# Cross attention of a two-layer decoder: the constant with which Pool rounds the probabilities, and the products that took it out again

## The reference, cut to what matters

```python
def _fq_unsigned(x, axis):
    s = jnp.max(x, axis=axis, keepdims=True) / 255.0
    s = jnp.maximum(s, 1e-08)
    q = jnp.clip(jnp.round(x / s), 0.0, 255.0) * s
...
attn = jnp.einsum('bhqd,bhkd->bhqk', q, k)
attn = jax.nn.softmax(attn.astype(jnp.float32), axis=-1)
attn = _fq_unsigned(attn, axis=-1)
out = jnp.einsum('bhqk,bhkd->bhqd', attn, v)
```

## Time and profile before

| | us |
|---|---|
| median of 3 runs | 1989.98 |
| their range | 1984.67 to 1989.99 |
| the profiled execution | 1981.8 |
| its span in the trace | 1980.1 |

### The profile page before, as it was taken

One profiled execution on the slowest core, in us unless ns is written; L12 is line 12 of the kernel. 1 busy time (PEld: TensorE's weight loads), 2 busy tenths in 40 slices (PEclk: granted clock), 3 DMA queues, 4 the chain that ended last, 5 costly groups with the idle time before them and its releaser, 6 DMA issues. The chain is left out here.

```text
span 1980.1 us, 38681 instructions
## 1 busy us (share of the span) xinstructions
PE 1809.8 (91%) x15222; PEld 968.5 (49%) x15222; DVE 1349.2 (68%) x2353; ACT 1131.5 (57%) x1657; POOL 970.0 (49%) x1021
## 2 busy tenths in 40 slices
PE   7988999979999999999999999999999578899698
PEld 3476788846665333333333333333333367666454
DVE  1454777775667999999999999999600353676622
ACT  2170556645623777777777777777777253766311
POOL 1010455559702878878787887878878010000000
PEclk9998999979999999999999999999999775999889
DMA  6002444457664111111111011100010240465000
GB/s 220 0 1 55 116 121 120 114 148 173 189 195 122 25 25 21 25 25 21 17 25 25 13 25 25 24 13 1 17 38 28 62 129 1 131 178 166 30 1 10
DMA packets 105395, 132.20 MB, mean 67 GB/s; under 512 B 9047, under 2 KB 94875, under 8 KB 104860
## 3 DMA queue, kind: packets, MB, share of 16 engines
q1 hardware_dynamic: 104364, 128.39, 24.7%
q10 hardware_dynamic: 864, 1.51, 0.2%
HBM read 89.78 MB, written 38.55 MB: 65 GB/s over the span
## 5 line engine op out<-in xcount | busy, mean ns | idle before, releaser
L1127 DVE TENSOR_REDUCE c_top<-c_ps 128x1 f32<-128x500 f32 x1344 | 827.7, 672 | 83.9 <-PE c_ps L875 36.3
L795 POOL TENSOR_SCALAR c_values<-c_values 125x896 f16<-125x896 f32 x768 | 721.5, 939 | 265.3 <-ACT c_values L1343 231.8
L1343 ACT ACTIVATE c_values<-c_ps 125x896 f32<-125x896 f32 x768 | 660.7, 915 | 238.3 <-PE c_ps L952 237.9
L964 PE MATMUL c_ps<-c_values,c_total 125*32 125x448 f32 x3072 | 369.0, 551 | 1.5 <-POOL c_values L795 1.5
L875 PE MATMUL c_ps<-kx,c_qx 64*128 64x500 f16 x1152 | 316.0, 386 | 24.6 <-DVE c_top L1127 15.0
L952 PE MATMUL c_ps<-c_qx,kx 64*125 64x448 f16 x1536 | 252.7, 362 | 4.1 <-ACT c_values L1343 3.9
L875 PEld LDWEIGHTS c_ps<-kx,c_qx 64*128 64x128 f16 x1152 | 82.3, 93 | 289.5 <-DVE c_top L1127 232.7
L815 PE MATMUL c_ps<-shared_w,c_rows 128*125 128x256 f32 x768 | 184.7, 384 | 0.0
L815 PEld LDWEIGHTS c_ps<-shared_w,c_rows 128*125 128x125 f32 x768 | 146.1, 190 | 24.4
L969 PE MATMUL c_ps<-c_values 125*16 125x448 f16 x1536 | 143.8, 352 | 0.0
L2009 POOL MEMSET f_select<- 8x1408 f32 x1 | 1.3, 1262 | 286.5 <-POOLq L1705 286.5
(11 more groups left out here) (275 smaller groups left out, 2158.7 us busy)
## 6 DMA issues: line engine op xcount, KB each, us to landing
c_rows<-in_ctx_T SPq DMA_DIRECT2D x96, 250.0 KB, 3.5
kx<-k_parts SPq DMA_DIRECT2D x192, 93.8 KB, 3.7
v<-c_halves SPq DMA_DIRECT2D x48, 265.6 KB
c_v<-v SPq DMA_DIRECT2D x16, 796.9 KB
k_parts<-c_parts SPq DMA_DIRECT2D x48, 250.0 KB, 2.6
k_T<-c_kback SPq DMA_DIRECT2D x48, 250.0 KB, 5.7
c_kT<-k_T SPq DMA_DIRECT2D x16, 750.0 KB
f_wgu<-in_f_Wgu SPq DMA_DIRECT2D x2, 1408.0 KB, 19.2
```

The source lines that it names most:

```text
L795: nc.gpsimd.tensor_scalar(probs[:, n % SLOTS], expo[:, n % SLOTS], ROUND_AT, 1.0, ALU.add, ALU.mult).then_inc(s["rounded"], 1)
L964: nc.tensor.matmul(ps[32 * g:32 * g + 32, 3, 0:TOKENS], total[:], expo[:, n % SLOTS, g % 2, :], start=(at == 0), stop=False, skip_group_ch ...
L1127: nc.vector.tensor_reduce(top[:, pair % 2, tile, at:at + 1], ring(n)[:, 0:BLOCK], AX.X, ALU.max)\
L1343: nc.scalar.activation(expo[:, n % SLOTS], ps[0:KP, 4 + 2 * (n % 2):6 + 2 * (n % 2), 0:TOKENS], ACT.Exp, scale=UNSCALE, bias=LN255).then_i ...
```

## The change

ROUND_AT becomes 3 * 2^22 = 12582912. Pool now adds it and subtracts it in the same instruction; between 2^23 and 2^24 the f32 numbers are 1 apart, so the addition rounds and the subtraction leaves the step itself, which is written as f16. As the steps carry no offset, Pool's 42 additions of V's steps, PE's 192 offset products with their weight loads, PE's wait for them, and DVE's fill of `offset` go.

```diff
-ROUND_AT = 1024.0
+ROUND_AT = float(3 << 22)
...
-        offset = sb("c0_offset", [KP, TOKENS], F16)
...
-                link = linker(pool, s["vlink"])
-
-                def sum_values(group):
-                    pool.wait_ge(cs["v_steps"], 8 * group + 8)
-                    if group == 0:
-                        pool.wait_ge(cs["stored"], (UNITS // 2) * 32)
-                    tiles = v_steps[:, 16 * group:16 * group + 16, :].rearrange("p (j a) n -> p j a n", a=2)
-                    link(nc.gpsimd.tensor_tensor(v_sums[:, group], tiles[:, 0], tiles[:, 1], ALU.add))
-                    for j in range(2, 8):
-                        link(nc.gpsimd.tensor_tensor(v_sums[:, group], v_sums[:, group], tiles[:, j], ALU.add))
-
...
-                for group in range(KT // 16):
-                    sum_values(group)
...
-                    nc.gpsimd.tensor_scalar(probs[:, n % SLOTS], expo[:, n % SLOTS], ROUND_AT, 1.0,
-                                            ALU.add, ALU.mult).then_inc(s["rounded"], 1)
+                    nc.gpsimd.tensor_scalar(probs[:, n % SLOTS], expo[:, n % SLOTS], ROUND_AT, ROUND_AT,
+                                            ALU.add, ALU.subtract).then_inc(s["rounded"], 1)
...
-                    if at % 8 == 7:
-                        if b == 7:
-                            pe.wait_ge(s["vlink"], 7 * (KT // 16))
-                        for g in range(4):
-                            h = 2 * pair + g % 2
-                            last = nc.tensor.matmul(ps[32 * g:32 * g + HD, 3, 0:TOKENS],
-                                                    v_sums[:, at // 8, g // 2, h * HD:(h + 1) * HD], offset[:],
-                                                    start=False, stop=True, skip_group_check=True)
...
-                nc.vector.memset(offset[:], -ROUND_AT).then_inc(s["side_ones"], 1)
...
-                    dve.wait_ge(s["side_ones"], 3)
+                    dve.wait_ge(s["side_ones"], 2)
```

More of the change, by code:

```diff
@@ L554, in layer0_cross_attention @@
         ctx_T = late(128, 0, 896).rearrange("p (c n) -> p c n", c=C2)
-        v_sums = parts[0:KP].rearrange("p s i c n -> p (s i c n)")[:, 0:6 * 2 * D]\
-            .rearrange("p (g a n) -> p g a n", g=6, a=2)
         w = k.sum_all[:, 0:2 * D].rearrange("p (c n) -> p c n", c=C2)
```

## The result

| | median us | runs | range |
|---|---|---|---|
| before | 1987.79 | 4 | 1984.67 to 1989.99 |
| after | 3518.41 | 4 | 3514.72 to 3521.26 |

The ratio is 1.770 (95% interval 1.766 to 1.773): the kernel takes 1531 us more, where 8 us less were forecast. It is the rival that had 3 in 100, at a price beyond the far bound.

A forecast was written before the change was run, and what follows sets the result against it. The prediction took a loop of PE and DVE handing banks to each other as the bound, with offset products in PE's link. Gains of 7.8 + 0.2 = 8.0 us took 1990.0 to 1982.0 us, range 1972 to 1988.

The forecast's parts named there:

- the rival that had 3 in 100: Layer 0's cross attention: slower roundings make Pool the bound; about 2630 us at 2.018 us a rounding; chance 0.03.
- the far bound: Highest price considered for Pool's new rounding: 2018 ns for 896 elements, at the pace of Pool's tensor_tensor.
- The rounding itself: Pool's add and subtract in one tensor_scalar: taken at 939 ns, the price of add with multiply for 125x896.
- The point from which Pool decides, 1.13 us: Price of a rounding from which Pool sets the step; each 0.1 us beyond costs 77 us.
- PE's offset products while both passes run: 41 groups in PE's loop with DVE, 0.19 us gained for each that goes: 7.8 us, between nothing and 12.3.
- the last group: Offset products at the second pass's end, which ACT's copy of the bank waits for: 0.19 us gained.
- The second pass alone: Six groups of offset products after the first pass, lying in a wait for ACT's exp: nothing, at most 1.1 us.
- The sums of V's steps: Pool's 42 additions, 48 us, ending before Pool's 82 us wait for ACT: dropping them gains nothing.
- the fill of offset: DVE's 0.43 us fill, absorbed by a later 1.05 us wait for Pool: nothing gained, at most 0.43 us.
- Hidden after all: PE catches up the offset products' delay, or another engine holds the steps at 4.58 us: 1990.0 us; chance 0.13.
- more than the link: DVE's whole 0.30 us wait returns at each group and small terms' covers are thin: 14.0 us, 1976.0 us; chance 0.04.
- wrong if L795's mean is over 1.13 us: Sign against the forecast: Pool's rounding line, expected to stay at 939 ns, averaging over 1.13 us.

The follow-up runs named there:

- e3_dropped_alone: Changed kernel with the old rounding back (Pool adds 1024, multiplies by 1.0), sums, offset products and fill still gone: 1980.6 us against 1985.7 for the kernel before, ratio 0.997.
- the four versions whose steps are 2^-24: Changed kernel with Pool rounding by a quick pair into steps of 2^-24, as f16 or int16, with various constants: 1985.4, 1982.9, 1983.4 and 1982.5 us.
- the last version: Version with two mults (2^-24 and 1.0, written as f16), its constants replaced by 1024 and 2^-34: 1982.5 us against 1986.7, ratio 0.9982.
- the version of add with 2^-24: Version with two mults (2^-24 and 1.0, written as f16), changed to add 0.0 and multiply by 2^-24: 1983.4 us against 1986.3, ratio 0.9984.

## Why the prediction was wrong

*The step that failed* is "The rounding itself", with its sentence "I take 939: the same instruction with one input and two operations on constants". The trace of before held no such pair, which the text said; the choice between the bounds leaned on shape and type, and the runs show that with both the same the price can be 3.4 times as high. The kind of the second operation, which the text named as the only thing that changes and counted as evidence against harm, was all of it: 937 or 3202 ns on the same operands (L797, L798). Both tensor_scalars that Pool ran before were add+mult, so the rows could show one kind alone.

*The far bound* was too near as well. It was taken from tensor_tensor, 2.25 ns an element (2018 / 896); the slow pair costs 3.6 (3225 / 896). A pace measured on another instruction was no upper end for this one.

*The rival's mechanism* was right, its price and its chance weren't. The point from which Pool decides, 1.13 us, and the cost beyond it describe three prices (0.94, 2.45 and 3.2 us) to within 35 us. At its far bound of 2018 ns the rival gave 2630 us; at the 3.168 us of spacing it gives 768 * 3.168 = 2433 us for the stage, which is the measured one.

*The other terms held.* PE's offset products while both passes run and the last group: 8.0 us forecast, 7.85 measured when they alone go, with steps of 4.53 us but for those at a pair's end. The second pass alone gave nothing. The sums of V's steps and the fill of offset hid nothing and cost nothing: the first rounding stayed (631.3 us before, 631.7 after), with Pool's wait before it grown from 82 to 143 us. *Hidden after all* and *more than the link* are both excluded by that run. In the changed kernel itself the 8 us can't be seen: with Pool as the bound they are PE time that nobody waits for. That e3_dropped_alone's 1980.6 us lie near the forecast 1982.0 is in part luck: the whole kernel gained 5.1 us and not 8.0, and the kernel before, at 1990.0 in the three runs from which the forecast started, took 1985.7 in the twelve runs beside that experiment.

*The sign that was named* was the right one: "wrong if L795's mean is over 1.13 us".

## What to carry to other kernels

An operation whose exact form is not in the trace has no price, however near its neighbours look: the kind of arithmetic can make an instruction 3.4 times as long on the same operands, so it should be timed alone before anything is hung on it. When an engine has little to spare in a loop (here 3.92 us of roundings in a step of 4.53), the question is not what an edit saves elsewhere but what it does to that engine, because a gain of 0.19 us a group was at stake here against 77 us for each 0.1 us of rounding. A quick instruction that leaves no gap can also cost: one instruction of seven elements on DVE came 0.03 us too late for it, and that took 5 of the 8 us.

## What the runs showed of the hardware

- On Pool a tensor_scalar of 125x896 takes 0.94 us as add+mult, mult+add or mult+mult, 2.45 us with a single operation and 3.20 us with every other pair tried, whatever the constants, the data and the output's type (f16 or f32; int16 with mult+mult alone).
- Two of them in a row start 1.02 us apart when 1024 is one of the constants (1536 has the same gap on half the tile) and 0.90 us apart with the other constants tried, at the same 0.94 us each; with the slow pair it is 3.28 against 3.17 us, 88 us over the kernel. No cause was found.
- DVE's copies and tensor_scalars of 128x7 in SBUF that started beside a quick rounding ended 0.03 us after it at the earliest: up to 0.94 us for what takes 0.17 us without one. Beside a slow rounding one took 0.17 us, well inside its 3.23 us.
- The stages behind the last copy of the bank took 443.0 us before (1980.1 - 1537.1), 444.7 with the offset products dropped (1974.4 - 1529.7) and 448.0 to 449.0 in the four versions whose steps are 2^-24, 448.9 in the last of them (1978.3 - 1529.4), in one execution each. PE's granted clock from 80 to 140 us behind that copy doesn't explain it: it was 0.57 in the last version, but 0.63 both with the products dropped and in the version of add with 2^-24 (below), whose stages behind took 448.0 us. Whether these us belong to the versions or to the executions wasn't tried; they are as large as half of a gain of 8 us.

The stretch and its busy times by engine, with the products dropped, in the last version, and in that of add with 2^-24:

```profile
1609.70:1669.70 60.00, 51.61 (x299) 47.93 (x299) 28.73 (x64) 30.31 (x133) 0.00 (x0) 0.63 0.09 29
```

```profile
1609.40:1669.40 60.00, 53.96 (x282) 51.22 (x281) 26.74 (x60) 29.51 (x128) 0.00 (x0) 0.57 0.09 27
```

```profile
1613.90:1673.90 60.00, 51.61 (x299) 47.74 (x299) 28.74 (x64) 30.51 (x134) 0.00 (x0) 0.63 0.09 28
```
